# Row maxima of three attentions, transposed in eight tiles of 32 queries into four PSUM banks and gathered by one copy, and ternary steps moved

## The reference

```python
x = x + attention16(layernorm(x), ctx, ctx) @ Wo + bo          # L0: 16 heads of width 16, 120 keys
x = x + ffn_ternary(layernorm(x))                              # w -> clip(round(w / mean|w|), -1, 1)
x = x + block(layernorm(x), ctx)                               # two _mha: a1 and a2
x = x + experts(x)                                             # 8 experts, the best one of each token

def _mha(x, y, ...):                                           # 16 heads of width 32
    q, k, v = ...                                              # a1: y = x, 256 keys; a2: y = ctx, 120 keys
    a = softmax(q @ k.T * D ** -0.5)                           # a1: multiplied by a causal mask afterwards
    x_out = x + (a @ v) @ li1_w + li1_b
    return x_out + gelu(ln(x_out) @ li2_w + li2_b) @ li3_w + li3_b

def _weight_quant(w):
    scale = 1.0 / clip(mean(abs(w)), 1e-05)
    return clip(round(w * scale), -1.0, 1.0) / scale
```

## Times and profile before

| | us |
|---|---|
| three runs | 1093.31, 1093.66, 1098.78 |
| median | 1093.66 |
| the profiled execution | 1098.47 |
| its span, first to last instruction | 1096.5 |
| mean granted clock of TensorE in it | 0.983 |
| L0 attention, first maxima transposes to last scores of it | about 37 to 132 of the span |
| a1 attention | about 317 to 477 |
| a2 attention | about 672 to 757 |

### The profile page before, as it was taken

The page is one execution under the profiler, slowest core; times in us unless marked ns, Lnnn a source line. Parts: engine busy times, 40 slices in busy tenths (PEclk is TensorE's granted clock), DMA queues, the critical chain, the costliest instruction groups (busy, mean ns, idle before and its releaser), DMA issues.

```text
span 1096.5 us, 21109 instructions
## 1 busy us (share of the span) xinstructions
PE 1019.6 (93%) x8670; PEld 741.8 (68%) x8679; DVE 542.7 (49%) x1309; ACT 439.9 (40%) x651; POOL 267.5 (24%) x409
## 2 busy tenths in 40 slices
PE   7888876999999989899999999999999999999997
PEld 4565553554457777776776566777578658999996
DVE  5466599987338888951522333885232143200000
ACT  6556554666445555543122224554221231121220
POOL 3021311011103434342122110666320102322311
PEclk9899998999999999999999999999999999999999
DMA  8600000000032000000000020000611217755410
GB/s 259 87 2 2 1 1 1 1 1 1 1 90 26 15 28 3 2 2 1 1 1 1 0 96 1 2 3 7 225 39 34 82 57 261 284 189 192 164 48 1
DMA packets 55360, 60.57 MB, mean 55 GB/s; under 512 B 23603, under 2 KB 47071, under 8 KB 55266
## 3 DMA queue, kind: packets, MB, share of 16 engines
q1 hardware_dynamic: 52322, 52.93, 15.9%
q0 software_dynamic: 2944, 6.30, 1.8%
HBM read 54.76 MB, written 7.21 MB: 57 GB/s over the span
## 4 chain that ended last, share of the span: by engine, by line
PE 81%; DVE 8%; ACT 5%; issue 3%; DMA 1%; POOL 1%; SPq 1%; POOLq 0%; DVEq 0%; ACTq 0%
PE ps L1879 15%; PE ps L2185 10%; PE ps L2327 8%; PE ps L2340 7%; PE ps L1815 6%; PE ps L1779 6%; PE ps L1748 4%; PE ps L2005 3%; PE ps L2260 3%; PE ps L1827 2%; PE ps L1745 2%; PE ps L1787 2%; PE ps L1822 2%; PE ps L1772 2%; PE ps L1686 2%
## 5 line engine op out<-in xcount | busy, mean ns | idle before, releaser
L830 DVE TENSOR_REDUCE small<-ps 128x8 f32<-128x960 f32 (+1 forms) x128 | 146.1, 1182 | 54.2 <-PE ps L1748 34.5
L1879 PE MATMUL ps<-r_w,r_k 128*128 128x256 f32 x512 | 113.2, 381 | 2.5 <-ACT r_k L1587 2.5
L2185 PE MATMUL ps<-r_a,r_w 128*128 128x512 f32 x256 | 112.0, 594 | 3.1 <-ACT r_a L1420 3.1
L1879 PEld LDWEIGHTS ps<-r_w,r_k 128*128 128x128 f32 x512 | 96.4, 190 | 18.6 <-issue 4.4
L1347 ACT ACTIVATE r_a<-ps 120x1024 f32<-120x1024 f32 (+1 forms) x80 | 77.5, 1021 | 76.8 <-PE ps L1787 76.8
L2185 PEld LDWEIGHTS ps<-r_a,r_w 128*128 128x128 f32 x256 | 48.2, 190 | 59.8 <-issue 56.0
L2327 PE MATMUL ps<-r_a,w_block 128*128 128x128 f32 x736 | 86.4, 275 | 1.0 <-ACT r_a L1648 1.0
L2327 PEld LDWEIGHTS ps<-r_a,w_block 128*128 128x128 f32 x736 | 85.6, 192 | 2.5 <-ACT r_a L1648 1.0
L1587 ACT ACTIVATE r_k<-ps,pvec 128x512 f32<-128x512 f32 x64 | 44.0, 687 | 101.0 <-PE ps L2185 101.0
L2340 PE MATMUL ps<-w_all,r_a 128*128 x368 | 83.2, 379 | 0.2 <-issue 0.2
L1656 ACT ACTIVATE r_a<-ps 128x512 f32<-128x512 f32 x46 | 27.5, 597 | 129.4 <-PE ps L2327 115.6
(11 more groups left out here) (278 smaller groups left out, 1855.4 us busy)
## 6 DMA issues: line engine op xcount, KB each, us to landing
w_block<-in_L_ffn_W SPq DMA_DIRECT2D x23, 1024.0 KB
w_all<-in_L_ffn_W SPq DMA_DIRECT2D x8, 1024.0 KB, 10.0
r_w<-in_L_xattn_a_li_w SPq DMA_DIRECT2D x4, 1024.0 KB, 7.2
x_rows<-x_all SPq DMA_DIRECT2D x4, 512.0 KB, 3.0
x_rows<-r_a SPq DMA_DIRECT2D x4, 512.0 KB, 3.0
x_all<-in_x SPq DMA_DIRECT2D x3, 512.0 KB, 6.2
y_all<-in_L_ffn_w_gate SPq DMA_DIRECT2D x1, 1024.0 KB, 8.7
y_all<-in_L_ffn_w_up SPq DMA_DIRECT2D x1, 1024.0 KB, 11.2
```

Of the source, the lines that this page charges most:

```text
L830: ins_ = dve.tensor_reduce(nm.rearrange("p (j s) -> p j s", j=4)[:, j:j + count, :], src, AX.X, ALU.max, negate=True)
L1879: ins_ = pe.matmul(o[:, t // 2, (t % 2) * D:(t % 2 + 1) * D], src[:, c, t * P:(t + 1) * P], w[:, c, :], start=(c == 0), stop=(c == chunks ...
L2185: ins_ = pe.matmul(o, LI[a]["li2"][:, c, m * P:(m + 1) * P], FT3[:, c, :], start=(c == 0), stop=(c == KC - 1))
```

## The change

The two transposes of 128 rows become eight: for each of the two query tiles t and each strip i of 32 partitions, one transpose of 32 queries by 128 columns into columns 32t to 32t+31 of key bank i. All four key banks are written, so the wait before it is for both exponentials of the unit before, and `banks_free` stands first in the first turn. The key scores have no wait of their own any more but the one for the copy, and all strips come behind it. The copy reads 64 columns from each of four banks and writes them in query order to maxT.

ScalarE calls `between(i)` right after max_copy(i), ahead of exponentials(i). The sums of absolute weights move from i = 0, 1, 2 to i = 1, 2, 3. The steps at 5, 8, 11 and 7, 10, 13 keep their numbers and so stand earlier in their turn. VectorE's bias subtraction moves from turn 0 to 3, its roundings from 6, 9, 12 to 7, 10, 13.

```diff
-        def max_bank():
-            return key_bank(2)
...
                 def rounding(i):
-                    if i == 0:
+                    if i == 3:
...
-                    if i in ROUND_AT:
-                        k = ROUND_AT.index(i)
+                    if i - 1 in ROUND_AT:
+                        k = ROUND_AT.index(i - 1)
...
                 def max_copy(n):
                     act.wait_ge(sem["maxT_done"], n + 1)
-                    act.activation(maxT[:], max_bank()[:, 0:S], ACT.Copy).then_inc(sem["maxT_ready"], 1)
+                    act.activation(maxT[:].rearrange("p (t i q) -> p i t q", t=T, i=4),
+                                   key_bank(0, 4)[:, :, 0:64].rearrange("p i (t q) -> p i t q", t=T), ACT.Copy).then_inc(sem["maxT_ready"], 1)
...
                             max_copy(FIRST[a] + i)
+                            between(i)
                             exponentials(FIRST[a] + i)
                         if i >= 1:
                             out_copy(FIRST[a] + i - 1)
-                        between(i)
                 def ternary(i):
-                    if i < 3:
-                        act.wait_ge(sem[f"q_loaded{i}"], 16)
-                        act.activation(tern[i], raw[i], ACT.Abs, accum_out=asum[:, i:i + 1]).then_inc(sem["wsum_ready"], 1)
+                    if 1 <= i <= 3:
+                        act.wait_ge(sem[f"q_loaded{i - 1}"], 16)
+                        act.activation(tern[i - 1], raw[i - 1], ACT.Abs, accum_out=asum[:, i - 1:i]).then_inc(sem["wsum_ready"], 1)
...
                     if n > FIRST[UNIT_OF[n][0]]:
-                        pe.wait_ge(sem["exp_done"], 2 * (n - 1) + 1)
+                        pe.wait_ge(sem["exp_done"], 2 * n)
                     for t in range(T):
-                        ins_ = pe.transpose(max_bank()[:, t * P:(t + 1) * P], MX[:, t, :], ident[:])
+                        for i in range(4):
+                            rows = slice(32 * i, 32 * i + 32)
+                            ins_ = pe.transpose(key_bank(i)[:, 32 * t:32 * t + 32], MX[rows, t, :], ident[rows, rows], tile_position=(32 * i, 0))
...
                 def keys_and_shifts(n):
-                    if n > FIRST[UNIT_OF[n][0]]:
-                        pe.wait_ge(sem["exp_done"], 2 * n)
-                    key_scores(n, (0, 1), 0)
                     pe.wait_ge(sem["maxT_ready"], n + 1)
-                    key_scores(n, (2, 3), 0)
+                    key_scores(n, (0, 1, 2, 3), 0)
                     key_scores(n, (2, 3, 0, 1), 1)
...
                     for n in range(n0 - 1, n1):
+                        if n == n0 - 1:
+                            banks_free()
                         if n + 1 < n1:
                             max_transposes(n + 1)
...
-                        if n == n0 - 1:
-                            banks_free()
```

## The result

The changed kernel takes 1090.43 us (median of ten runs, 1085.97 to 1092.41) against 1094.46 us for the kernel before on the same chip (ten runs, 1093.31 to 1098.78). The ratio is 0.9952 with a 95% interval of 0.9935 to 0.9969: about 5 us less, 4 by the medians. The forecast was 1093.6, no change; the rival "clock holds" said 1088.1. Single executions of 1723 to 3688 us, of the kernel before and of three experiments, are left out of medians and ratios.

A forecast was written before the change was run, and what follows sets the result against it. TensorE is four fifths of the chain that ended last, so time is won only where it stands still. L0 -4.7, a1 +3.2, a2 +1.4 made -0.1 us, applied to the median 1093.66: 1093.6 us, 80% range 1087 to 1099.5.

The forecast's parts named there:

- clock holds: First rival, chance 0.23: the granted clock does not fall in L0's unit 1 and long units; -5.6 us, 1088.1 us.
- Edit 1: L0: ternary steps behind the maxima copy fit ScalarE's pause with 0.1 to 0.2 us left; the copy is no longer late.
- Edit 2: L0 units 7, 10, 13: ScalarE's step and exponentials wait for VectorE's moved rounding; these units become 6.61 us.
- Edit 3: T, start of a unit's maxima transposes, waits for both exponentials: loop of 4.93 us in L0, 4.98 in a1; a2 unchanged.
- The sign of wrong: a1 units at 4.81 us, against about 4.90 forecast, would show that the second exponential wasn't late.
- Edit 4: Eight transposes take 0.26 us against 0.20; 0.03 comes off the loop in L0, 0.08 in a1, 0 in a2.
- second rival: Chance 0.15: small transposes follow at 0.06 us each, L0 and a1 units become 5.09; +5.7 us, 1099.3 us.
- Edit 5: Start of each attention: bank wait ahead of the first transposes makes T(1) later, +1.60 us in L0, +1.12 in a1 and a2.
- +3.0 for falls: L0: two of the three new 6.61 us units were expected to fall in clock, for 1.60 and 1.38 us.
- a fall worth 2.46: L0's unit 1: the clock was expected to fall again, 4.90+2.46 = 7.36 us, -1.04 against before.
- +0.25 at its end: Last unit of each attention: four more key loads and a copy 0.1 us later, +0.25 us.

The follow-up runs named there:

- e4: Kernel before with the maxima transposes waiting for both exponentials of the unit before, not the first only: 1097.0 us, ratio 1.0012.
- e7: Changed kernel with the eight small transposes issued twice, one block behind the other: 1087.7 us, ratio 0.9935 to the kernel before.
- e12: Changed kernel with ScalarE's out copy behind the copy of the maxima instead of ahead of it: 1113.1 us, ratio 1.0158 to the kernel before.
- e15: Changed kernel with VectorE's product of the attended values in a1 cut from 256 columns to 8: 1087.9 us, ratio 0.9925 to the kernel before.
- e1: Kernel before with only the ternary steps and the rounding moved as in the change; old transposes and waits stay: 1087.2 us, ratio 0.9916.
- e3: Changed kernel with VectorE's rounding put back in the turn it had before: 1085.3 us, ratio 0.9906 to the kernel before.
- e2: Changed kernel with ternary steps and rounding put back; eight transposes, gathering copy and new waits stay: 1096.7 us, ratio 1.0018 to the kernel before.
- e5: Kernel before with the wait for free banks ahead of the first maxima transposes of each attention: 1094.3 us, ratio 0.9988.

## Why the prediction was right or wrong

The time came out inside the stated range, partly by luck. The mechanism held for L0 (edits 1 and 2) and failed for a1 and for the start of a2; errors of several us cancelled in the sum and again on the way from the profiled execution to the median. The forecast was no change, and the change gains 4 to 5 us.

**Edit 1** right: copy in time, steps hidden. Units 2 to 4 were forecast at 15.7 and take 15.80 (48.51 to 64.31), though one by one they are off by 0.28, 0.28 and 0.10 (4.62, 5.48, 5.70 for 4.90, 5.20, 5.6).

**Edit 2** right in mechanism and nearly in size: 6.61 against 6.42, 7.14 and 6.57. What it lacked is GpSimd's addition in unit 10: the rounding there takes 1.91, not 1.28. The prediction never asked what GpSimd does beside the moved rounding.

**Edit 3** is the step that failed for a1 ("a new loop arises", +0.09 a unit, +1.8). I took 2.92, a distance between two times in the kernel before, for a path that T starts. e4 shows that T can come later without moving the exponentials, e7 that more work behind T does not either. The sign of wrong that the prediction named, a1 at 4.81, came true, but not for its reason ("the second exponential wasn't late"): T does wait for it, and what follows does not wait for T. The loop that decides runs through the out copy (e12), which the prediction had named, as the third strip's wait, and then used only as a cover.

**Edit 4** mis-sized and harmless: 0.13 instead of 0.26 for eight transposes, and scores at T+0.09 for T+0.26. The idle 0.17 behind the transposes is gone and 0.36 to 0.43 stay in front of them, as the prediction said. Its chain to the copy (T+0.61) was too long: the copy starts at T+0.39 in a1, behind the out copy. The second rival (1099.3) falls with e7: even sixteen do not cost it. The copy took 0.38, as assumed.

**Edit 5** right for L0 in the time, by two misses that cancel: T(1) was forecast at 42.46 and is at 42.40, but T(0) comes 0.38 later than forecast (37.94 for 37.56) and the exponentials stand at T(0)+2.40, not +2.84. Wrong in sign for a2: T(0) to T(2) is 9.90 (663.07 to 672.97) against 11.75, which outweighs a T(0) that comes 1.3 later. The prediction priced the later T(1) and did not look at the clock of the unit behind it, 0.72 in the kernel before. In a1 it is 9.79 against 11.45, and T(0) starts 1.3 after the last product ahead of it, as in a2; in the kernel before it starts together with that product.

**Clock.** The +3.0 for falls in two of the long units did not come: the twelve long units in the profiled executions of the change, e7, e12 and e15 (6.41 to 7.14) and the three of e1 (5.52 to 6.24) all ran at 1.00. In unit 1 of L0 the forecast was a fall worth 2.46. The change shows 0.72 and 6.11 us, a fall worth 1.5 beside e3, which has the same code there and shows 1.00 and 4.61. The first rival ("clock holds") is right for the long units; in unit 1 the forecast is nearer (a fall in six of the nine kernels with the banks first).

**The sum on the profiled pair.** L0, forecast -4.7, is -10.1 to its last T: clock 3.0, unit 1 1.25 (6.11 for 7.36), the other seven units behind T(5) 1.3 (33.09 for 34.39: in the two units behind a long one and in unit 14 the out copy ends at T+0.16 or T+0.36, in units 5 and 6 at T+0.54), against 0.3 more in the long ones; the +0.25 at its end lies in the next stretch. a1, forecast +3.2, is +0.65 (+2.19 up to its T(0), -1.54 within): the 1.8 for its units is missing, and its second unit kept the clock. Of the 2.19, 1.3 is the later T(0); in the same stretch the mean clock is lower (0.955 for 0.964), which nobody forecast. a2, forecast +1.4, is -0.7 with the rest of the kernel (+1.3, -1.9, -0.1). Together -10.1 for -0.1.

**From profile to median.** I carried the sum to the median unchanged. But the profiled execution of before held falls of the clock worth 1.60+1.38 in scaled units and 2.46 in unit 1, and most runs of that kernel show a mean clock near 0.988, not its 0.983. Of the twelve scaled units in the profiled executions of before, e2, e4 and e5, which all keep the steps ahead of the copy, five ran below full clock, not two of three. So a median run has fewer falls to lose. A sum that was right on the pair, -10.1, carried over unchanged, would have given 1083.5, 6.9 us too low. The two errors, the gain too small on the profile and the transfer too direct, partly cancelled: 1093.6 is 3.2 us above the measured median. That is luck.

## What to carry to other kernels

A distance read between two events is a path only if moving the first moves the second; before pricing a wait, look for the transfer or copy whose end keeps a constant distance to what follows in all units. A step moved to cover itself must be checked against what each other engine does in its new turn, the engine with which it shares a port included; where an engine has little slack in a loop, cut the operation into pieces that fit that slack. And before a sum worked out on one profiled execution is carried to a median, its clock falls have to be priced apart.

## What the runs showed of the hardware that was not expected

- A VectorE tensor_scalar of 128x2048 in float32 beside GpSimd: 1.19 us free, 1.91 when issued during GpSimd's addition; GpSimd's product 0.73 free, 1.62 to 1.71 when issued during the rounding.
- Transposes of 32x32 in four row strips: sixteen loads put the next loads 0.13 us later than eight, 0.016 each.
- Same code, same stretch, another clock: L0's unit 1 took 6.11 us in the change (granted clock 0.72) and 4.61 in e3 (1.00). The ten runs of the change go with it: 1085.97 us at a mean granted clock of 0.993, 1092.41 at 0.985.
